# The inverse of a 32x32 triangular factor: four levels of two products against five stages of one, on the tiles of TensorE

## The chip, the cores and the metric

The kernel is one program on one core of a Trainium2 chip. The metric is the device time of one execution in microseconds (us), lower is better. TensorE (PE) multiplies, VectorE (DVE), ScalarE (ACT) and GpSimd (POOL) work element by element, SyncE (SP) issues transfers. Everything is float32.

## What is computed

A time-mixing layer of the RWKV kind over 2 sequences of 4096 tokens with 512 channels, and then eight experts over its 8192 rows. What matters here is the recurrence of each of the 16 heads (width 32):

```python
def step(S, inp):
    r_, w_, k_, v_, kk_, b_ = inp
    sab = jnp.einsum('bhvk,bhk->bhv', S, kk_)
    S = S * jnp.exp(w_)[:, :, None, :] + sab[..., None] * b_[:, :, None, :] + v_[..., None] * k_[:, :, None, :]
    y = jnp.einsum('bhvk,bhk->bhv', S, r_)
    return (S, y)
```

Since `sab` of a token depends on the states of all tokens before it, a chunk of 32 tokens is solved at once: with L the strictly triangular 32x32 matrix of the scores between `kk` and `b`, the inverse of a unit triangular matrix made of L is needed for each head and chunk.

## The kernel before

The program has two parts. `time_mix` runs until about 4600 us of the profile, `experts` after it; the change touches the first alone. `time_mix` takes 128 rows in a turn (64 tokens of each of the two sequences), so there are 64 tiles. Four stages of different tiles share a turn: N and A (norm, projections), B (scores of the tile before), C (solving and the state of the tile before that) and D (output). `LONG` = 28 turns are written out in a loop body that runs twice, with some turns ahead of it and behind it. A turn has 16 units (`U`: 4 channel groups x 2 sequences x 2 chunks), and each unit 4 heads, which lie on the four groups of 32 partitions (`head(h)`). A small product of one head thus takes one 32x32 tile of the PE array, the one in row group h and column group h.

The order of each engine is written by hand. `DVE_STEPS`, `ACT_STEPS`, `POOL_STEPS` and `PE_STEPS` list the steps of a turn, each engine counts them with a semaphore, and `on_vector`, `on_scalar`, `on_gpsimd` and `on_tensor` issue in that order and wait for counts of the others. A name such as C.P0 is a step of stage C. `Banks` lists who uses which of the eight PSUM banks in turn; `clear` waits for the last reader.

The inverse in a turn before:

- Stage B leaves `ub` (L, turned), `invT` (the identity with the first pairs filled in under a mask) and `inv` (`invT` turned).
- For each of four levels, `P_of` (L849) computes 64 products of 32x32 by 32 columns into bank 6, ACT copies them to `part` (L605), `Q_of` (L860) computes 64 more into bank 7, DVE copies those entries that the level adds into `invT` under a mask (L402, C.T) and turns the result into `inv` (L406, C.I; not after the last level). P and Q are each issued in two halves of 32 products with other PE work between.

Every float32 product is two records in the profile, so a half is 64 records. Between the halves stand the steps that the prediction follows: `value_of` (L825), "centre" (L964), "mix" (L972), "rated" (L978), "var" (L990, which reads D.squares of ACT, L644), "delta" (L929), `low` for gate1, low_wa and low_k (L834), `key_of` (L825), the scores u0 to u5 and y0 to y5 (`score`, L874), "decay" (L1053), low2 (L1069) and `from_values` (L888). DVE takes the scores out of PSUM under the mask of known keys (`mask_scores`, L377), into one tile `raw`. D.gated (L484) is the DVE step that frees the bank of u1. PE runs at `from_values` into both banks of the inverse.

## Time and profile before

| | |
|---|---|
| median of 3 runs | 6516.54 us (6496.91 to 6517.45) |
| the profiled execution | 6509.57 us, span of its instructions 6507.4 us |
| PE busy | 5869.2 us (90%), 135752 matrix products |
| DVE busy | 3906.5 us (60%) |
| ACT busy, POOL busy | 1874.9 us (29%), 937.7 us (14%) |
| mean granted TensorE clock | 0.973 of 2.4 GHz |

A busy engine is one with an instruction in flight. A row of the timeline gives when a group of like instructions starts, how long it lasts to the end of its last instruction, and in brackets the idle time before it with who ended it; "issue" stands for idle time for which the profile shows no wait. PE's products overlap, so the time that a group takes of PE is read from its start to the start of the next group.

### The profile page before, as it was taken

How to read it: one execution, taken by the hardware profiler on the slowest of the kernel's cores; microseconds unless marked ns; L12 is line 12 of the kernel's file. 1: busy time of each engine (PE TensorE's matmuls, PEld its weight loads, DVE VectorE, ACT ScalarE, POOL GpSimd, SP SyncE). 2: the span in 40 equal slices, each digit the busy share in tenths (PEclk: the TensorE clock that was granted, in tenths of full speed). 3: DMA queues.
4: the chain of work that ended last, by engine and by line, in shares of the span. 5: the costliest groups of instructions: out<-in, count | busy, mean ns of one | idle time of the engine just before them, and what ended most of it. 6: DMA issues, size and time to landing. Idle time of an engine off the chain costs nothing. (4 is left out here: it accounts for less than half of the span.)

```text
span 6507.4 us, 293913 instructions
## 1 busy us (share of the span) xinstructions
PE 5869.2 (90%) x135752; PEld 4180.8 (64%) x135752; DVE 3906.5 (60%) x9323; ACT 1874.9 (29%) x3531; POOL 937.7 (14%) x900
## 2 busy tenths in 40 slices
PE   6888988998988888898888988987499999999999
PEld 5777777777777777777777777776244444444443
DVE  5777777777777777777777777775523323322300
ACT  3333333333333333333333333332000000000000
POOL 0111111111111111111111111110202202220210
PEclk9999999999999999999999999998699999999999
DMA  1000000000000000000000000000211211121120
GB/s 57 21 18 17 23 17 18 23 17 17 23 17 17 23 18 17 22 19 17 23 18 17 24 17 17 24 15 14 90 46 66 73 65 60 60 92 46 66 71 13
DMA packets 108833, 214.34 MB, mean 33 GB/s; under 512 B 25424, under 2 KB 26704, under 8 KB 107088
## 3 DMA queue, kind: packets, MB, share of 16 engines
q1 hardware_dynamic: 92240, 144.98, 7.6%
q0 software_dynamic: 15360, 50.48, 2.3%
q8 instruction: 1073, 17.58, 1.1%
q14 instruction: 160, 1.31, 0.1%
HBM read 144.67 MB, written 50.72 MB: 30 GB/s over the span
## 5 line engine op out<-in xcount | busy, mean ns | idle before, releaser
L377 DVE COPY_PREDICATED time_raw<-time_known,w_bank 128x96 f32<-128x96 int32 (+6 forms) x3072 | 823.5, 274 | 240.3 <-PE w_bank L874 151.9
L1661 PE MATMUL moe_bank<-moe_w,moe_hidden 128*128 128x512 f32 x2048 | 928.7, 596 | 0.0
L1648 PE MATMUL moe_bank<-moe_hT,moe_w 128*128 128x512 f32 x2048 | 924.8, 594 | 0.8 <-DVE moe_hT L1548 0.8
L1648 PEld LDWEIGHTS moe_bank<-moe_hT,moe_w 128*128 128x128 f32 x2048 | 386.8, 191 | 472.3 <-issue 471.1
L1661 PEld LDWEIGHTS moe_bank<-moe_w,moe_hidden 128*128 128x128 f32 x2048 | 379.4, 190 | 429.5 <-issue 428.1
L1569 ACT ACTIVATE moe_hidden<-moe_bank,moe_b 128x512 f32<-128x512 f32 x256 | 175.9, 687 | 1628.2 <-PE moe_bank L1648 1522.9
L860 PE MATMUL w_bank<-time_invT,time_part 32*32 32x32 f32 x32768 | 418.7, 196 | 141.1 <-issue 88.2
L860 PEld LDWEIGHTS w_bank<-time_invT,time_part 32*32 32x32 f32 x32768 | 372.4, 107 | 201.3 <-issue 138.5
L849 PE MATMUL w_bank<-time_inv,time_ub 32*32 32x32 f32 x32768 | 412.6, 196 | 72.9 <-issue 38.7
L849 PEld LDWEIGHTS w_bank<-time_inv,time_ub 32*32 32x32 f32 x32768 | 355.0, 107 | 190.4 <-issue 149.9
L802 POOL TENSOR_TENSOR time_tail<-time_tail,time_lp 128x512 f32<-128x512 f32 x64 | 75.4, 1178 | 2777.8 <-ACT time_lp L732 2682.9
L874 PE MATMUL w_bank<-time_keys,time_queries_u 32*32 32x160 f32 x8192 | 356.4, 300 | 49.5 <-DVE time_mixed L484 35.0
L874 PE MATMUL w_bank<-time_keys,time_queries_y 32*32 32x160 f32 x8192 | 350.7, 302 | 36.8 <-issue 18.7
L402 DVE COPY_PREDICATED time_invT<-time_levels,w_bank 128x512 f32<-128x512 int32 x256 | 186.9, 730 | 307.4 <-PE w_bank L860 307.2
L1548 DVE COPY moe_hT<-moe_bank 128x512 f32<-128x512 f32 x64 | 44.2, 691 | 535.5 <-PE moe_bank L1635 535.5
L874 PEld LDWEIGHTS w_bank<-time_keys,time_queries_y 32*32 32x32 f32 x8192 | 251.4, 106 | 125.2 <-issue 74.9
L392 DVE SCALAR_TENSOR_TENSOR time_lerp<-w_bank,time_maa,time_xx 128x128 f32<-128x128 f32 x1024 | 284.8, 341 | 54.8 <-PE w_bank L929 54.6
L874 PEld LDWEIGHTS w_bank<-time_keys,time_queries_u 32*32 32x32 f32 x8192 | 239.1, 105 | 89.3 <-DVE time_mixed L484 41.1
L609 ACT COPY time_corr<-w_bank 128x256 f32<-128x256 f32 x128 | 47.6, 372 | 853.6 <-PE w_bank L912 853.6
L825 PE MATMUL w_bank<-time_xf,time_key_w 128*128 128x128 f32 x2048 | 290.6, 292 | 1.8 <-ACT time_part L605 0.7
L825 PE MATMUL w_bank<-time_xf,time_value 128*128 128x128 f32 x2048 | 288.5, 291 | 0.1
L825 PE MATMUL w_bank<-time_xf,time_receptance 128*128 128x128 f32 x2048 | 280.1, 285 | 0.8 <-issue 0.8
(225 smaller groups left out, 9716.9 us busy)
## 6 DMA issues: line engine op xcount, KB each, us to landing
moe_w<-in_w SPq DMA_DIRECT2D x64, 1024.0 KB, 7.2
mid_xn<-time_xn_rows SPq DMA_DIRECT2D x128, 129.0 KB, 2.7
time_x_rows<-in_x SPq DMA_DIRECT2D x128, 128.0 KB, 2.9
time_base<-in_x SPq DMA_DIRECT2D x128, 128.0 KB, 3.2
mid_acc<-time_mixed SPq DMA_DIRECT2D x128, 128.0 KB, 2.7
mid_scores<-time_rated SPq DMA_DIRECT2D x128, 2.0 KB, 1.7
moe_b<-in_b SPq DMA_DIRECT2D x8, 256.0 KB
time_receptance<-in_w_receptance SPq DMA_DIRECT2D x1, 1024.0 KB, 4.9
```

Source lines behind the costliest of these rows:

```text
L377: e.copy_predicated(by_raw[:, "uy".index(q), n0:n1, :, 0:8 * j + 8], known[:, "uy".index(q), :, :, mine].to_broadcast([P, n1 - n0, 2, 8 * ...
L392: e.scalar_tensor_tensor(grp(lerp, g), grp(BANK[f"delta{f}"], g), wt["maa"][:, f * G + g:f * G + g + 1], grp(xx, g), ALU.add, ALU.mult).th ...
L402: e.copy_predicated(chunks(got["invT"]), level(lev + 1, U), chunks(BANK[f"Q{lev}"])).then_inc(dve.sem, dve.step(f"C.T{lev}"))
L609: e.copy(col(corr), BANK[f"solve.{n}{c}"][:, 0:SU * N]).then_inc(act.sem, act.step(f"C.{n}{c}"))
L802: e.tensor_tensor(chunks(tail), chunks(tail), padded(lp)[:, :, 1:33], ALU.add).then_inc(pool.sem, pool.step("A.lt"))
L825: mm = e.matmul(ps[:, o * P:(o + 1) * P], weight[:, g * width + o * P:g * width + (o + 1) * P], rhs_of(g), start=g == 0 and (o == 0 or not ...
L849: mm = e.matmul(BANK[f"P{lev}"][head(h), blk(n)], got["ub"][head(h), blk(n)], got["inv"][head(h), blk(n)], start=True, stop=True, skip_gro ...
L860: mm = e.matmul(BANK[f"Q{lev}"][head(h), blk(n)], part[head(h), blk(n)], got["invT"][head(h), blk(n)], start=True, stop=True, skip_group_c ...
L874: mm = e.matmul(BANK[f"{q}{m}"][head(h), (n - n0) * 2 * KEYS:(n - n0 + 1) * 2 * KEYS], queries[q][head(h), blk(n)], keys[head(h), n * 2 * ...
L1569: e.activation(hidden[now % 4][:, :], up[now % 3][:, :], ACT.Gelu_apprx_tanh, bias=b1[:, x * FC + k:x * FC + k + 1]).then_inc(act.sem, act ...
L1648: got = e.matmul(up[now % 3][:, :], w1[:, g * F + k * P:g * F + (k + 1) * P], hT[x % 2][:, g * CAP + half * HALF:g * CAP + (half + 1) * HA ...
L1661: got = e.matmul(down[t][:, :], hidden[now % 4][:, t * P:(t + 1) * P], tile(w2, k), start=k == 0, stop=k == FC - 1)
```

## The change

The inverse is made by another recurrence. With A the unit triangular matrix and W the inverse so far, the pair [E | W] with E = W A is multiplied from the left by 2I - E, which gives both the next E and the next W. Stage B leaves W = I - L (`sum_of(ew)`, turned from `raw`, whose first quarter now starts as the identity) and 2I - W, which is E for the start (`rest_of(ew)`), the latter on POOL (B.e1). Five stages k = 1, 2, 4, 8, 16 follow. Stage 1 makes E alone (32 moving columns a product), stages 2, 4 and 8 make both (64 columns), stage 16 makes W alone (32 columns). Each stage has 64 products, in two halves again, written over both banks 6 and 7. Between two stages ACT copies the banks to `ew` (C.S), DVE turns the E part into `grow` (C.t), and POOL subtracts it from twice the identity (C.b); the last stage is copied to `invT` by ACT.

In stages 2 and 8 the products of units 8 to 15 write their result two column groups on, and stages 4 and 16 read them there. Their tiles are (row group h, column group h + 2) beside (h, h). The units are issued in the order 0, 8, 1, 9, and so on.

Removed are all P and Q products, `part`, the masks `levels` and their DVE copies, four DVE transposes (three C.I and B.inv), and POOL's copy of the identity (B.eye).

```diff
-            def invert(lev):
-                e.wait_ge(pe.sem, pe[f"C.Q{lev}"])
-                e.copy_predicated(chunks(got["invT"]), level(lev + 1, U), chunks(BANK[f"Q{lev}"])).then_inc(
-                    dve.sem, dve.step(f"C.T{lev}"))
-                if lev < 3:
-                    e.wait_ge(dve.sem, dve[f"C.T{lev}"])
-                    e.transpose(col(got["inv"]), col(got["invT"])).then_inc(dve.sem, dve.step(f"C.I{lev}"))
+            def turn_rest(k):
+                if k == 1 and c_was:
+                    e.wait_ge(pe.old, pe.ago("C.S16"))
+                e.wait_ge(act.sem, act[f"C.S{k}"])
+                e.transpose(chunks(grow), rest_of(got["ew"])).then_inc(dve.sem, dve.step(f"C.t{k}"))
...
+            if Cs:
+                turn_rest(8)
+            if Bs:
                 e.wait_ge(dve.sem, dve["B.u5.3"])
-                e.transpose(col(out["ub"]), raw_of(0)).then_inc(dve.sem, dve.step("B.ub"))
-            if Cs:
-                invert(3)
-            if Bs:
-                e.wait_ge(pool.sem, pool["B.eye"])
-                e.wait_ge(dve.sem, dve["B.ub"])
-                e.copy_predicated(chunks(out["invT"]), level(0, U), chunks(out["ub"])).then_inc(
-                    dve.sem, dve.step("B.pairs"))
-                e.wait_ge(dve.sem, dve["B.pairs"])
-                e.transpose(col(out["inv"]), col(out["invT"])).then_inc(dve.sem, dve.step("B.inv"))
+                e.transpose(sum_of(out["ew"]), chunks(raw_of(0))).then_inc(dve.sem, dve.step("B.ub"))
...
+            def inverse_of(k):
+                e.wait_ge(pe.sem, pe[f"C.S{k}"])
+                if k == 1:
+                    e.copy(rest_of(got["ew"]), rest_of(both_banks)).then_inc(act.sem, act.step("C.S1"))
+                elif k == 16:
+                    e.copy(chunks(invT), sum_of(both_banks)).then_inc(act.sem, act.step("C.S16"))
+                else:
+                    e.copy(col(got["ew"]), inv_bank).then_inc(act.sem, act.step(f"C.S{k}"))
...
+            def grow_of(k):
+                e.wait_ge(dve.sem, dve[f"C.t{k}"])
+                e.tensor_tensor(chunks(grow), every_unit(wt["eye2"]), chunks(grow), ALU.subtract).then_inc(
+                    pool.sem, pool.step(f"C.b{k}"))
...
+            def inverse_stage(k, half):
+                if half == 0:
+                    clear(e, f"S{k}")
+                    clear(e, f"S{k}+")
+                    if k == 1:
...
+                        e.wait_ge(pool.old, pool.ago("B.e1"))
+                    else:
+                        e.wait_ge(pool.sem, pool[f"C.b{k // 2}"])
+                taken = {1: slice(0, N), 16: slice(N, 2 * N)}.get(k, slice(0, 2 * N))
+                by = raw_of(0) if k == 1 else grow
+                for i in range(half * HALF_U // 2, (half + 1) * HALF_U // 2):
+                    for n in (i, i + HALF_U):
+                        turned_in = TURN * (n // HALF_U) * (k in (4, 16))
+                        turned_out = TURN * (n // HALF_U) * (k in (2, 8))
+                        for h in range(HG):
+                            rows, to = head((h + turned_in) % HG), head((h + turned_out) % HG)
+                            mm = e.matmul(both_banks[to, n * 2 * N + taken.start:n * 2 * N + taken.stop], by[rows, blk(n)],
+                                          got["ew"][rows, n * 2 * N + taken.start:n * 2 * N + taken.stop],
+                                          start=True, stop=True, skip_group_check=True)
+                if half:
+                    mm.then_inc(pe.sem, pe.step(f"C.S{k}"))
```

On PE the first place is the start of a turn: mix (L972), rated (L978), the first Q halves (L860) with a part of value (L825) between, var (L990) and delta (L929) before.

```order
L972 MATMUL w_bank<-time_lerp,time_maa_w 128x128 x4
L978 MATMUL w_bank<-time_gcent,time_x 64x8 x8
L860 MATMUL w_bank<-time_invT,time_part 32x32 x32
L825 MATMUL w_bank<-time_xf,time_value 128x128 x4
L860 MATMUL w_bank<-time_invT,time_part 32x32 x32
L990 MATMUL w_bank<-time_sq,time_head_ones 128x512
L929 MATMUL w_bank<-time_mix,time_maa_w 128x128 x12
L825 MATMUL w_bank<-time_hid_g,time_gate_w 128x128 x4
L849 MATMUL w_bank<-time_inv,time_ub 32x32 x32
```

After the change, the same place on PE (mix is L991, rated L997, var L1005, delta L948, a stage's half L879):

```order
L991 MATMUL w_bank<-time_lerp,time_maa_w 128x128 x4
L997 MATMUL w_bank<-time_gcent,time_x 64x8 x8
L847 MATMUL w_bank<-time_xf,time_value 128x128 x4
L1005 MATMUL w_bank<-time_sq,time_head_ones 128x512
L948 MATMUL w_bank<-time_mix,time_maa_w 128x128 x12
L847 MATMUL w_bank<-time_hid_g,time_gate_w 128x128 x4
L879 MATMUL w_bank<-time_ew,time_grow 32x64 x32
```

Both Q halves are gone ahead of var, and the half of P behind the gate has become a half of stage 2 with 64 columns.

The second place is the end of the inverse on PE, from the decay (L1053 before, L1057 after) to the scores y (L874, L894) and from_values (L888, L907). Before:

```order
L1053 MATMUL w_bank<-time_hid_w,time_decay_w 128x128 x4
L849 MATMUL w_bank<-time_inv,time_ub 32x32 x32
L874 MATMUL w_bank<-time_keys,time_queries_u 32x160 x16
L860 MATMUL w_bank<-time_invT,time_part 32x32 x32
L1069 MATMUL w_bank<-time_hid,time_low_w 128x128 x16
L860 MATMUL w_bank<-time_invT,time_part 32x32 x32
L874 MATMUL w_bank<-time_keys,time_queries_y 32x160 x24
L888 MATMUL w_bank<-time_by_values,time_vT 32x96 x32
```

After:

```order
L1057 MATMUL w_bank<-time_hid_w,time_decay_w 128x128 x4
L879 MATMUL w_bank<-time_ew,time_grow 32x64 x32
L894 MATMUL w_bank<-time_keys,time_queries_u 32x160 x16
L879 MATMUL w_bank<-time_ew,time_grow 32x32 x32
L1073 MATMUL w_bank<-time_hid,time_low_w 128x128 x16
L879 MATMUL w_bank<-time_ew,time_grow 32x32 x32
L894 MATMUL w_bank<-time_keys,time_queries_y 32x160 x24
L907 MATMUL w_bank<-time_by_values,time_vT 32x96 x32
```

The order reads alike, but the halves after the scores u4 and u5 (L894, x16) are now stage 16, which reads `grow` of stage 8, where the halves of Q3 read `part` of ACT.

The third place is POOL over a turn. Before (L780 B.rk, L783 B.eye, L771 the queries, L767 C.faded, L802 A.lt, L808 and L813 B.us and B.ys):

```order
L780 TENSOR_TENSOR time_rk<-time_r,time_k 128x512 [waits mix_go_pool,pe_steps2,dve_steps2,act_steps2,pool_steps2]
L783 COPY time_invT<-time_eye 128x512 [waits pe_steps2]
L771 TENSOR_TENSOR time_queries_u<-time_dq,time_kkn 128x512 [waits pe_steps2,dve_steps2,act_steps3]
L771 TENSOR_TENSOR time_queries_y<-time_dq,time_r 128x512 [waits pe_steps2,act_steps2,act_steps3]
L767 TENSOR_TENSOR time_faded<-time_state,time_decay_end 128x256 [waits act_steps2,dve_steps2]
L802 TENSOR_TENSOR time_tail<-time_tail,time_lp 128x512 [waits act_steps3]
```

After:

```order
L796 TENSOR_TENSOR time_rk<-time_r,time_k 128x512 [waits mix_go_pool,pe_steps2,dve_steps2,act_steps2,pool_steps2]
L787 TENSOR_TENSOR time_queries_u<-time_dq,time_kkn 128x512 [waits pe_steps2,dve_steps2,act_steps3]
L783 TENSOR_TENSOR time_grow<-time_eye,time_grow 128x512 [waits dve_steps3]
L787 TENSOR_TENSOR time_queries_y<-time_dq,time_r 128x512 [waits pe_steps2,act_steps2,act_steps3]
L778 TENSOR_TENSOR time_faded<-time_state,time_decay_end 128x256 [waits act_steps2,dve_steps2]
L783 TENSOR_TENSOR time_grow<-time_eye,time_grow 128x512 [waits dve_steps3] x3
L820 TENSOR_TENSOR time_ew<-time_eye,time_ew 128x16x32 [waits dve_steps3]
L824 TENSOR_TENSOR time_tail<-time_tail,time_lp 128x512 [waits act_steps3]
```

POOL has lost the copy of the identity and has four subtractions into `grow` (L783) and one into `ew` (L820); the first stands ahead of the y queries.

## Rows read from the trace of the kernel before

**Rows 1.** The page, DMA queues: the queue of instructions, packets, MB, share

```profile
q8 instruction: 1073, 17.58, 1.1%
```

**Rows 2.** One line's instructions (L953, a turn's first), 674 to 4310 us

```profile
L953 PE MATMUL w_bank<-time_ident,time_xn_rows x212: 272/273/445, 674.5 to 4300.1; 128*128 128x128 f32 x106
```

**Rows 3.** Timeline of PE, one turn: start, length, work, [idle before <-releaser]

```profile
2853.30 1.12 PE L990 MATMUL w_bank<-time_sq,time_head_ones 128*128 128x512 f32 x2
...
2865.81 1.02 PE L874 MATMUL w_bank<-time_keys,time_queries_u 32*32 32x160 f32 x24 [0.66 <-DVE time_mixed L484]
2867.28 0.74 PE L849 MATMUL w_bank<-time_inv,time_ub 32*32 32x32 f32 x64 [0.46 <-DVE time_inv L406]
2869.01 1.13 PE L834 MATMUL w_bank<-time_xf,time_low_k 128*128 128x128 f32 x8 [0.99 <-DVE time_xf L398]
2870.07 0.75 PE L849 MATMUL w_bank<-time_inv,time_ub 32*32 32x32 f32 x64
2870.76 2.05 PE L825 MATMUL w_bank<-time_xf,time_key_w 128*128 128x128 f32 x16
```

**Rows 4.** Timeline of PE, the end of the inverse in that turn

```profile
2879.75 0.60 PE L849 MATMUL w_bank<-time_inv,time_ub 32*32 32x32 f32 x47
2881.33 0.34 PE L849 MATMUL w_bank<-time_inv,time_ub 32*32 32x32 f32 x17 [0.98 <-issue]
2881.51 1.29 PE L874 MATMUL w_bank<-time_keys,time_queries_u 32*32 32x160 f32 x32
2882.60 0.78 PE L860 MATMUL w_bank<-time_invT,time_part 32*32 32x32 f32 x64
2883.34 0.71 PE L1069 MATMUL w_bank<-time_hid,time_low_w 32*128 32x128 f32 x12
2884.92 0.94 PE L1069 MATMUL w_bank<-time_hid,time_low_w 32*128 32x128 f32 x20 [0.87 <-issue]
2885.79 0.75 PE L860 MATMUL w_bank<-time_invT,time_part 32*32 32x32 f32 x64
2886.40 2.39 PE L874 MATMUL w_bank<-time_keys,time_queries_y 32*32 32x160 f32 x48
2888.57 1.55 PE L888 MATMUL w_bank<-time_by_values,time_vT 32*32 32x96 f32 x64
```

**Rows 5.** Timeline of PE: 64 records of 64 columns on four tiles

```profile
2903.99 1.09 PE L902 MATMUL w_bank<-time_by_state,time_state 32*32 32x64 f32 x64
2905.01 2.05 PE L825 MATMUL w_bank<-time_xf,time_receptance 128*128 128x128 f32 x16
```

**Rows 6.** Timeline of DVE, the same turn

```profile
2842.94 1.33 DVE L423 TENSOR_TENSOR time_grown<-time_grown,time_shrink 128x256 f32<-128x256 f32 x1
2844.30 0.71 DVE L427 TENSOR_TENSOR time_state<-time_grown,time_faded 128x256 f32<-128x256 f32 x1
...
2865.67 0.72 DVE L402 COPY_PREDICATED time_invT<-time_levels,w_bank 128x512 f32<-128x512 int32 x1
2866.42 0.71 DVE L406 STREAM_TRANSPOSE time_inv<-time_invT 128x512 f32<-128x512 f32 x1
...
2882.32 2.07 DVE L377 COPY_PREDICATED time_raw<-time_known,w_bank 128x32 f32<-128x32 int32 x8 [1.30 <-PE w_bank L874]
...
2900.97 0.43 DVE L423 TENSOR_TENSOR time_grown<-time_grown,time_shrink 128x256 f32<-128x256 f32 x1
```

**Rows 7.** Timeline of ACT, the same turn

```profile
2850.77 0.58 ACT L644 ACTIVATE time_sq<-w_bank 128x512 f32<-128x512 f32 x1
...
2886.87 0.61 ACT L702 ACTIVATE time_thmk<-w_bank 128x512 f32<-128x512 f32 x1
```

**Rows 8.** Timeline of POOL, the same turn

```profile
2852.00 1.19 POOL L771 TENSOR_TENSOR time_queries_u<-time_dq,time_kkn 128x512 f32<-128x512 f32 x1 [7.26 <-ACT time_dq L647]
```

**Rows 9.** Busy time by windows: PE, PEld, DVE, ACT, POOL, then PE's granted clock

```profile
2003.60:2007.00 3.40, 2.43 (x55) 2.02 (x42) 3.40 (x8) 0.96 (x2) 0.00 (x0) 1.00 0.00 0
2007.00:2010.40 3.40, 3.11 (x80) 2.86 (x84) 2.20 (x7) 2.86 (x6) 0.58 (x1) 0.50 0.02 5
```

More of the change, by code:

```diff
@@ L214, in time_mix @@
         eights = lambda t: t[:, :].rearrange("p (n j s) -> p n j s", n=U, j=BLOCKS)
-        level = lambda i, n: wt["levels"][:, blk(i)].rearrange("p (o t) -> p o t", o=1).to_broadcast([P, n, N])
+        every_unit = lambda t: t[:, :].rearrange("p (o t) -> p o t", o=1).to_broadcast([P, U, N])
+        pairs_of = lambda t: t[:, :].rearrange("p (n s t) -> p n s t", n=U, s=2)
+        rest_of = lambda t: pairs_of(t)[:, :, 0]
+        sum_of = lambda t: pairs_of(t)[:, :, 1]
+        inv_bank = both_banks[:, :]
         FILLS = {"x": x, "lp": lp, "state": state, "raw": raw, "bank4": psum[4], "bank5": psum[5]}
-        dve.stage([*FILLS, "pad", "hid_w", "ones"] + [f"bonus_ones{g}" for g in range(G)]
+        dve.stage([*FILLS, "pad", "hid_w", "ones", "raw_eye"] + [f"bonus_ones{g}" for g in range(G)]
                   + [f"bias_ones{g}" for g in range(G)] + ["gcent", "offset"])
@@ L459, in on_vector @@
             if Cs:
-                invert(0)
+                turn_rest(1)
             if A:
@@ L780, in on_gpsimd @@
                 e.tensor_tensor(col(rk), col(r), col(k2), ALU.mult).then_inc(pool.sem, pool.step("B.rk"))
-                if "C.y1" in pe.was:
-                    e.wait_ge(pe.old, pe.ago("C.y1"))
-                e.tensor_copy(chunks(out["invT"]), wt["eye"][:, :].rearrange("p (o t) -> p o t", o=1).to_broadcast(
-                    [P, U, N])).then_inc(pool.sem, pool.step("B.eye"))
                 e.wait_ge(act.sem, act["B.eq"])
@@ L799, in on_gpsimd @@
                 faded_of(0)
+                grow_of(2)
+                grow_of(4)
+                grow_of(8)
+            if Bs:
+                e.wait_ge(dve.sem, dve["B.ub"])
+                e.tensor_tensor(rest_of(out["ew"]), every_unit(wt["eye2"]), sum_of(out["ew"]), ALU.subtract).then_inc(
+                    pool.sem, pool.step("B.e1"))
             if A:
@@ L845, in P_of @@
                     else:
-                        e.wait_ge(dve.sem, dve[f"C.I{lev - 1}"])
-                for n in range(half * U // 2, (half + 1) * U // 2):
-                    for h in range(HG):
-                        mm = e.matmul(BANK[f"P{lev}"][head(h), blk(n)], got["ub"][head(h), blk(n)], got["inv"][head(h), blk(n)],
-                                      start=True, stop=True, skip_group_check=True)
-                if half:
-                    mm.then_inc(pe.sem, pe.step(f"C.P{lev}"))
@@ L854, in Q_of @@
-            def Q_of(lev, half):
-                if half == 0:
-                    clear(e, f"Q{lev}")
-                    e.wait_ge(act.sem, act[f"C.P{lev}"])
-                for n in range(half * U // 2, (half + 1) * U // 2):
-                    for h in range(HG):
-                        mm = e.matmul(BANK[f"Q{lev}"][head(h), blk(n)], part[head(h), blk(n)], got["invT"][head(h), blk(n)],
-                                      start=True, stop=True, skip_group_check=True)
-                if half:
-                    mm.then_inc(pe.sem, pe.step(f"C.Q{lev}"))
+                        e.wait_ge(pool.sem, pool[f"C.b{k // 2}"])
@@ L1171, in time_mix_inputs @@
     t = row % N
-    same = lambda size: t // size == i // size
-    upper = {h: same(2 * h) & (t // h == i // h - 1) for h in (1, 2, 4, 8, 16)}
     f32 = lambda a: np.ascontiguousarray(a.astype(np.float32))
```

102 lines of the change are left out of this document (45 added, 57 removed), and 8 rows, old and new, of the table DVE_STEPS.

## The prediction, made before the changed kernel ran

> **What bounds the kernel now.** I read the rows of a turn's first line [rows 2], the timeline of each engine over one turn, and the windows with the granted clock. 212 records of L953, four to a turn, are 53 turns; (4300.1 - 0.4 - 674.5) / 52 = 69.7 us is a turn. I walk through the one that starts at 2841.18, 69.1 us long. From from_values on, at 2888.57 [rows 4], PE runs nearly without a wait to the end of the turn. Before it, PE meets waits: for D.gated ahead of u1 (0.66), for the turned inverse (0.46), for a mixed input (0.99) [rows 3], and "issue" gaps of 0.98 and 0.87 [rows 4]. Between resuming at 2881.33 and stopping at 2884.05 pass 2.7 us, so dense small products outrun the fetch. So PE bounds the end of the turn, and a chain over all engines its first two thirds. A saving on PE counts only where that chain gets shorter too.
>
> **What PE saves.** A half with 32 columns is 64 records in 2870.76 - 2870.07 = 0.69 us [rows 3]. Before there are 16 halves: 11.0 us. After there are 10. Four (stages 1 and 16) have 32 columns: 2.8 us. Six have 64 columns, which the trace shows on four tiles alone: 2905.01 - 2903.99 = 1.02 us [rows 5]. On eight tiles no row shows them. The lower end is half of 1.02, 0.51, if the tiles are all that counts; but 32 columns, half the streaming of 64, took 0.69 and not 0.51, so something per record holds as well. I take 0.69, the rate at which PE already gets through 64 records. That makes 4.1, and the sum 6.9 us: 4.1 less a turn. With 1.02 it is 8.9: 2.1 less.
>
> The pages speak both ways here. In the Trainium skill, "TensorE: Matmul & The Clock Gate", Part 3 (The mechanism), a weight load overlaps a product in flight only if it goes to another row group; the added tiles share their row groups with the old ones, so by that rule nothing would be gained from them, and six halves would stay at 1.02. Its section on measured speedup has sixteen tiles 10.6 times as fast as one, rows and columns together. No row here settles it; the rule is the first rival.
>
> **The chain, joint by joint.** Times are those of the turn in the rows, on eight tiles.
>
> *var.* POOL's copy of the identity is gone. L427 took 0.71 beside it, and the same kind of add over 256 columns takes 0.43 (L423, alone) [rows 6], so DVE runs 0.3 earlier into the mixing. With both Q halves gone, PE reaches var at about 2849.8, but var reads the squares of ACT, over at 2850.77 + 0.58 = 2851.35 [rows 7], now 0.3 earlier: var starts at 2851.15 instead of 2853.30 [rows 3], 2.15 earlier, behind a wait of 1.3.
>
> *u1.* From var to D.gated nothing of the chain (delta, the inputs, low_wa, ACT's affine) gets shorter: it moves 2.15. The first subtraction of POOL (1.19, as L771 [rows 8]) is over before the gate's products are, and costs nothing. Two POOL operations beside DVE cost something: L423 took 1.33 beside POOL's first operation of the turn and 0.43 alone [rows 6]; a DVE operation with both inputs in SBUF seems to wait for POOL. The first input's add (L398) falls on the y queries and loses some 0.6, still ahead of its use. u1 starts at 2863.6 instead of 2865.81. Q1a and Q1b no longer lie around u0, so PE waits about 2 us there in sum.
>
> *Stage 4.* Before, P starts 1.5 after D.gated is over (copy 0.72, transpose 0.71, latency). Now a transpose and a subtraction, 0.65 + 1.2, precede it: 1.9. It starts at 65.5 instead of 67.28 [rows 3], 1.8 earlier.
>
> *u4.* From there to u4 were 2881.51 - 2867.28 = 14.2 us. Two Q halves go (1.4), the wait of 0.99 goes as the input now comes first, the issue gap of 0.98 goes as the dense stretch is thinner, and a wait of 0.3 for POOL ahead of stage 8 is new: 11.1. u4 starts at 76.6, 4.9 earlier.
>
> *Stage 16: the new wait.* Q3 started at once behind u5 [rows 4], since ACT had its input. Stage 16 needs `grow` of stage 8, and C.t8 stands on DVE behind all masks of u4 and u5. These end 2882.32 + 2.07 - 2881.51 = 2.9 after u4 starts [rows 4, 6]; then transpose (0.65) and subtraction (1.2) with latencies: 4.85. PE has 1.1 us of scores for that time and idles 3.7 us. Queued behind are stage 16, low2, all y scores and from_values. Stage 16 starts at 81.45 instead of 2882.60: of 4.9 us, 1.15 are left.
>
> *from_values.* Before, 2888.57 - 2882.60 = 6.0 us passed for Q3a, low2, Q3b, y0 and y1 [rows 4], with a gap of 0.87 in low2 and more in the scores. Without gaps a half takes 0.69, low2 some 1.2 (20 of its 32 records took 0.87), and y0 and y1 1.63 (32 records of u4 and u5 took 1.09, these are 48): 4.2 in sum. ACT's last copy stands behind three activations (to 2887.48 [rows 7], 1.7 after low2) and ends 2.2 after low2, as PE does. from_values would start at 85.65, 2.9 earlier. After the long wait the next packet of instructions has been fetched, but four more dense groups follow; I give back 0.65 for gaps: 2.25 us a turn. Behind it everything moves along; the freed 2.9 us of DVE and ACT's longer copies (over two banks) lie beside PE.
>
> **The clock.** In 2003.6 to 2007.0 PE was busy 2.43 of 3.40 us, and in the next 3.4 us it was granted 0.50, 1.2 instead of 2.4 GHz; over the whole execution the mean is 0.973, so some 5% of the time is at half clock already [rows 9]. With 3.7 us idle in one piece each turn, and 2 to 3 us around u0, u1 and stage 4, I expect such a stretch about every turn behind the first and in half of the turns at the second. One of 3.4 us costs up to 1.7 where PE binds, less where the wait or a gap of the fetch covers it: 0.7 and 0.5 on average, 1.2 in sum. The skill's same page, Part 1, likewise lets idle stretches bring the clock down, and the rows agree (0.50 after 2.43 busy of 3.40).
>
> **Sum.** 2.25 - 1.2 = about 1.0 us a turn, over 64 turns 64 us. From the profiled execution's own 6509.6 us that is 6445; it is 7 us below the median, so I forecast 6452 us for the median, 1.0% faster.
>
> **Rivals.**
> 1. *The added tiles don't run beside the old ones.* Six halves at 1.02 instead of 0.69, all on the chain (two before low_wa, two around low_k, two ahead of u4): 2.0 us a turn more, minus 1.0 becomes plus 1.0: 6516 + 64 = 6580 us, 1% slower. It decides as soon as a 64-column half takes over 0.86 us. For it: no row shows two tiles on one row group, and a page's rule. Against it: nothing in the rows.
> 2. *The waits cost what PE saves.* If the clock falls in every turn at both places with its full 1.7, hardly covered, 3.4 instead of 1.2 is paid, and the gain is over: about 6520 us. For it: 2.43 us busy of 3.40 were few enough. Against it: the second stretch lies before a wait that partly absorbs it.
> 3. *PE binds all the way.* If the waits that I count are covered (the profile's 90% busy PE speaks for it), all 4.1 us arrive: 64 x 4.1 = 262 us, 6254 us. Against it: C.t8 cannot come before the masks of u5.
> 4. *No clock loss.* The chain as walked with 2.25 us: 6516 - 144 = 6372 us.
>
> **Numbers.** Forecast with its surroundings (6400 to 6495): 0.45; rival 1: 0.25; rival 2: 0.14; rival 3: 0.05; rival 4: 0.11. The range that leaves out rival 3 and the tails is 6365 to 6590. A measurement of this kernel tells some 0.3% from no change, so faster means below 6497 and slower above 6536: 0.58 faster, 0.14 the same, 0.28 slower.
>
> **What would show it.** Stage halves with 64 columns 0.6 to 0.7 us apart (rival 1: 1.0). PE idle ahead of stage 16 near 3.7 us, released by POOL's subtraction; ahead of var near 1.3, released by ACT's squares. from_values 44 to 46 us after the turn's first record instead of 47.4. Mean clock of the execution 0.95 to 0.97 instead of 0.973. A turn of 68.7 us instead of 69.7. Wrong it would be if the subtractions on POOL take much longer than 1.2 us, if the issue gaps stay as before, or if the clock stays low for long stretches.

## The result: 2.1% slower, and the profile after

| | before | after |
|---|---|---|
| median | 6516.99 us (6496.91 to 6521.21, 4 runs) | 6649.51 us (6633.48 to 6659.95, 4 runs) |
| ratio, 95% interval | | 1.0207 [1.0177, 1.0238] |
| span of the profiled execution | 6507.4 us | 6631.5 us |
| PE busy | 5869.2 us, 135752 products | 5824.3 us, 111176 products |
| DVE, ACT, POOL busy | 3906.5, 1874.9, 937.7 us | 3675.6, 1990.0, 1312.2 us |
| mean granted clock | 0.973 | 0.925 |

The forecast was 6452 us with a range of 6365 to 6590, so the sign was wrong and the time lies outside the range. 24576 PE records are gone and PE's busy time has hardly moved. Before any explanation, the place: the two kernels differ in the turns alone. The first line of a turn, one row of each kernel (min/median/max length, first and last start):

```profile
L953 PE MATMUL w_bank<-time_ident,time_xn_rows x256: 272/273/472, 32.0 to 4370.1; 128*128 128x128 f32 x128
```

```profile
L972 PE MATMUL w_bank<-time_ident,time_xn_rows x256: 272/273/473, 31.7 to 4491.7; 128*128 128x128 f32 x128
```

The last turn starts 121.6 us later, of 124.1 us that the span is longer. Over 63 turns that is 1.93 us a turn; the forecast had 1.0 us less.

The waits of PE that ended between 700 and 4300 us, in the kernel after (line that waited, who released it: us in total, times, longest):

```profile
PE w_bank L879 <- POOL time_grow L783: 233.4, 150, 3.7
PE w_bank L894 <- DVE time_mixed L493: 93.8, 51, 1.8
PE w_bank L1005 <- ACT time_sq L652: 63.9, 50, 1.4
PE w_bank L879 <- issue: 25.6, 45, 1.1
...
PE w_bank L847 <- ACT time_sq L658: 10.9, 38, 0.3
```

The first row is a stage that waits for POOL's subtraction, 150 times in 50 turns, the longest 3.7 us: the wait before stage 16. The second is u1 waiting for D.gated, the third "var" waiting for the squares. All three were named ahead, with about these sizes. So the waits alone don't explain the loss, and one has to go through a turn. Timeline of PE in the kernel after, one turn that starts at 2698.47 (rows between them left out):

```profile
2708.48 1.10 PE L1005 MATMUL w_bank<-time_sq,time_head_ones 128*128 128x512 f32 x2 [1.39 <-ACT time_sq L652]
...
2710.96 1.16 PE L847 MATMUL w_bank<-time_hid_g,time_gate_w 128*128 128x128 f32 x8 [0.29 <-ACT time_sq L658]
2712.05 0.85 PE L879 MATMUL w_bank<-time_ew,time_grow 32*32 32x64 f32 x64
2712.83 1.16 PE L847 MATMUL w_bank<-time_xf,time_value 128*128 128x128 f32 x8
...
2718.66 1.02 PE L894 MATMUL w_bank<-time_keys,time_queries_u 32*32 32x160 f32 x24
2721.52 1.82 PE L894 MATMUL w_bank<-time_keys,time_queries_u 32*32 32x160 f32 x24 [1.84 <-DVE time_mixed L493]
2723.57 1.17 PE L879 MATMUL w_bank<-time_ew,time_grow 32*32 32x64 f32 x64 [0.23 <-POOL time_grow L783]
2724.67 2.08 PE L856 MATMUL w_bank<-time_xf,time_low_k 128*128 128x128 f32 x8
2726.67 1.18 PE L879 MATMUL w_bank<-time_ew,time_grow 32*32 32x64 f32 x64
...
2736.87 1.29 PE L894 MATMUL w_bank<-time_keys,time_queries_u 32*32 32x160 f32 x32
2741.84 1.03 PE L879 MATMUL w_bank<-time_ew,time_grow 32*32 32x32 f32 x64 [3.67 <-POOL time_grow L783]
2742.79 2.09 PE L1073 MATMUL w_bank<-time_hid,time_low_w 32*128 32x128 f32 x32
2744.81 0.68 PE L879 MATMUL w_bank<-time_ew,time_grow 32*32 32x32 f32 x40
2745.74 0.43 PE L879 MATMUL w_bank<-time_ew,time_grow 32*32 32x32 f32 x24 [0.24 <-issue]
2745.95 3.10 PE L894 MATMUL w_bank<-time_keys,time_queries_y 32*32 32x160 f32 x48
2748.86 1.34 PE L907 MATMUL w_bank<-time_by_values,time_vT 32*32 32x96 f32 x56
```

Three things stand in it. A half with 64 columns on eight tiles takes 2712.83 - 2712.05 = 0.78 us. Behind the wait of 1.84 everything is slow: the same 24 records of scores take 1.82 instead of the 1.02 of the row above, low_k 2.00 us instead of 1.06 [rows 3]. Behind the wait of 3.67 it is the same, with low2 at 2.02 and the y scores at 2.91. The windows of this turn (PE, PEld, DVE, ACT, POOL busy, then PE's granted clock) name the cause:

```profile
2721.30:2728.10 6.80, 6.35 (x161) 4.96 (x162) 6.47 (x20) 0.84 (x3) 1.25 (x1) 0.50 0.01 2
2728.10:2741.80 13.70, 9.56 (x248) 8.15 (x247) 8.21 (x26) 3.48 (x5) 2.64 (x3) 1.00 0.01 3
2741.80:2748.60 6.80, 6.52 (x201) 5.69 (x205) 0.60 (x3) 3.65 (x8) 1.11 (x1) 0.50 0.02 5
```

In this turn PE was granted 1.2 GHz instead of 2.4 for 6.8 us behind each of the two long waits. Over the 58 turns from the fifth to the 62nd there is such a stretch in 57 turns at the first place and in all 58 at the second. They last 3.4 or 6.8 us, a few 10.2: per turn 5.0 us at the first place and 6.3 at the second. In all it is 12.5 us a turn against 2.5 before. The forecast had foreseen a stretch "about every turn" at the first place and in half of the turns at the second, and took one of 3.4 us for its price [rows 9].

The chain behind the wait of 3.67, on DVE and on POOL:

```profile
2737.68 2.07 DVE L387 COPY_PREDICATED time_raw<-time_known,w_bank 128x32 f32<-128x32 int32 x8 [0.96 <-PE w_bank L894]
2739.65 0.70 DVE L415 STREAM_TRANSPOSE time_grow<-time_ew 128x512 f32<-128x512 f32 x1
```

```profile
2740.43 1.26 POOL L783 TENSOR_TENSOR time_grow<-time_eye,time_grow 128x512 f32<-128x512 f32 x1 [6.23 <-DVE time_grow L415]
```

Masks of u4 and u5, transpose, subtraction, as walked ahead: u4 at 2736.87, stage 16 at 2741.84.

**The joints.** Where the groups of a turn start, in us into the turn, averaged over the fifth to the 62nd turn of each kernel (58 turns). Single turns differ, so that a mean at the late joints is known to some 0.2 us. The third column is the move that the prediction gave, before its 1.2 for the clock:

| | before | after | forecast | measured |
|---|---|---|---|---|
| var | 11.42 | 9.97 | -2.15 | -1.45 |
| low_wa | 19.27 | 18.53 | -2.15 | -0.74 |
| stage 4 (P of the third level) | 25.75 | 25.51 | -1.8 | -0.24 |
| u4 | 39.81 | 38.59 | -4.9 | -1.22 |
| stage 16 (Q of the last level) | 41.55 | 43.65 | -1.15 | +2.10 |
| from_values | 47.55 | 50.22 | -2.25 | +2.67 |
| end of the turn | 69.69 | 71.68 | -2.25 | +1.99 |

The rest of the turn, behind from_values, became 0.7 us shorter (22.14 and 21.46); PE's idle time in it fell from 0.9 to 0.4 us. The loss against the forecast lies in four joints: ahead of var, var to low_wa, stage 4 to u4, and stage 16 to from_values.

### The profile page after: what moved, and what is told of

It is laid out like the page before. It is cut to its first block and busy times, and to the rows that moved or that the text cites. A ratio compares the mean times of both kernels' runs of the same rounds, so it can differ in the third digit from the quotient of the medians.

```text
span 6631.5 us, 244569 instructions
## 1 busy us (share of the span) xinstructions
PE 5824.3 (88%) x111176; PEld 4057.1 (61%) x111176; DVE 3675.6 (55%) x9004; ACT 1990.0 (30%) x3595; POOL 1312.2 (20%) x1156
## 5 line engine op out<-in xcount | busy, mean ns | idle before, releaser
L879 PE MATMUL w_bank<-time_ew,time_grow 32*32 32x64 f32 x32768 | 482.9, 243 | 334.0 <-POOL time_grow L783 310.0
L879 PEld LDWEIGHTS w_bank<-time_ew,time_grow 32*32 32x32 f32 x32768 | 395.8, 120 | 456.4 <-issue 429.7
L783 POOL TENSOR_TENSOR time_grow<-time_eye,time_grow 128x512 f32<-128x512 f32 x256 | 323.0, 1262 | 1580.9 <-DVE time_grow L415 1580.9
L894 PE MATMUL w_bank<-time_keys,time_queries_u 32*32 32x160 f32 x8192 | 378.3, 317 | 121.7 <-DVE time_mixed L493 113.3
L894 PE MATMUL w_bank<-time_keys,time_queries_y 32*32 32x160 f32 x8192 | 407.1, 344 | 16.9 <-DVE time_mixed L553 12.1
L894 PEld LDWEIGHTS w_bank<-time_keys,time_queries_y 32*32 32x32 f32 x8192 | 294.2, 123 | 116.9 <-issue 50.3
L894 PEld LDWEIGHTS w_bank<-time_keys,time_queries_u 32*32 32x32 f32 x8192 | 244.1, 110 | 189.9 <-DVE time_mixed L493 133.2
L847 PE MATMUL w_bank<-time_xf,time_key_w 128*128 128x128 f32 x2048 | 273.6, 289 | 0.0
L847 PEld LDWEIGHTS w_bank<-time_xf,time_key_w 128*128 128x128 f32 x2048 | 249.6, 199 | 23.8 <-issue 20.5
L963 PE MATMUL w_bank<-time_output,time_mixed 128*128 128x512 f32 x512 | 256.0, 623 | 3.9 <-DVE time_mixed L493 3.9
```

The costliest lines, as they stand in the source:

```text
L783: e.tensor_tensor(chunks(grow), every_unit(wt["eye2"]), chunks(grow), ALU.subtract).then_inc(pool.sem, pool.step(f"C.b{k}"))
L847: mm = e.matmul(ps[:, o * P:(o + 1) * P], weight[:, g * width + o * P:g * width + (o + 1) * P], rhs_of(g), start=g == 0 and (o == 0 or not ...
L879: mm = e.matmul(both_banks[to, n * 2 * N + taken.start:n * 2 * N + taken.stop], by[rows, blk(n)], got["ew"][rows, n * 2 * N + taken.start: ...
L894: mm = e.matmul(BANK[f"{q}{m}"][head(h), (n - n0) * 2 * KEYS:(n - n0 + 1) * 2 * KEYS], queries[q][head(h), blk(n)], keys[head(h), n * 2 * ...
L963: mm = e.matmul(BANK["out"][:, :], grp(mixed, g), wt["output"][:, g * C:(g + 1) * C], start=g == 0, stop=g == G - 1)
```

## Experiments

Theory at this point: the tiles work and the waits are as forecast, but the price of the clock was put too low, and behind the wait for stage 16 PE runs at the pace of its instruction fetch, which the time saved ahead doesn't shorten. Rivals: the added tiles bring nothing; the clock alone; POOL as the culprit. Times are compared within the kernels that share their runs of the kernel before, or by the ratios to it (1% is 65 us). Averages are over the same 58 turns.

**e1_four_tiles**: the tiles of before, all else as changed.

```diff
-TURN = 2
+TURN = 0
```

> The changed kernel with all units on the tiles (h, h): the turn by two column groups is set to 0, so four tiles instead of eight. In the trace of the changed kernel a half with 64 columns takes 0.78 us on eight tiles, against 1.02 for such products on four. My theory (the tiles do run side by side, and the six halves lie on the chain) expects halves of 1.02 to 1.05 us and 6 x 0.25 = 1.5 us a turn more, less what the waits ahead of u1 and stage 8 absorb: 0.8 to 1.5 us over 64 turns, 50 to 95 us slower than the changed kernel (6700 to 6745 us). The rival, that the halves are bound by something else than the tiles or lie in the waits' cover, expects no change (within 15 us).

Measured: 6735.18 us, ratio 1.0301 [1.0283, 1.0318], 0.94% above the changed kernel (61 us; between the profiled executions 102 us). The first stage with 64 columns and the group behind it, timeline of PE:

```profile
1752.10 1.10 PE L879 MATMUL w_bank<-time_ew,time_grow 32*32 32x64 f32 x64
1753.13 1.16 PE L847 MATMUL w_bank<-time_xf,time_value 128*128 128x128 f32 x8
```

1.03 us a half, as rows 5 had it, against 0.78 on eight tiles. So the second set of tiles does run beside the first, and rival 1 of the prediction falls. The Trainium skill ("TensorE: Matmul & The Clock Gate", Part 3, The mechanism) has weight loads overlap with products in flight only where the row group differs; read strictly, eight tiles would have stayed at 1.03, and these two kernels don't agree with it. They don't reach half of 1.03 either. The loss is within the 50 to 95 us that were expected.

**e2_fill16** and **e3_fill_both**: PE gets unused products during its waits, which need no data that is late, so that it isn't idle there. e2 puts three products of 512 columns ahead of stage 16; e3 has in addition 512 and 256 columns between u0 and u1. Nothing else changes; their results are never read.

```diff
+            def fill(*columns):
+                clear(e, "mk")
+                for n in columns:
+                    e.matmul(BANK["mk"][:, 0:n], wt["head_ones"][:, :], xf[0][:, 0:n], start=True, stop=True)
...
+                if A and Cs:
+                    fill(512, 256)
...
+            if A and Cs:
+                fill(512, 512, 512)
```

> The changed kernel with three products of 128x128 by 128x512 (1.06 us each) into an idle PSUM bank, their results unused, put on PE into the wait of 3.67 us ahead of stage 16. They add no work to the chain. Theory clock: the wait itself was forecast right; what came on top is the half clock that follows it. Then low2 goes from 2.02 to about 1.1 us, y0 and y1 from 2.8 to 1.7, and the kernel gains 1.5 to 2.2 us a turn, 95 to 140 us (6510 to 6555 us). Theory wait: the time behind the wait is late input or fetch of instructions, which the added products leave or make worse: no gain, or up to 30 us slower.

> As the run before, and in addition one product with 512 and one with 256 columns (1.6 us) between u0 and u1, where PE waits 1.84 us. Theory clock: the second half-clock stretch of a turn, from u1 to the key product, goes too: stage 4's halves from 1.1 to 0.78 us, low_k from 2.0 to 1.1, about 1.3 us a turn and 60 to 90 us less than the run before (6430 to 6490 us), the mean clock over the turns back at 0.97 or more. Theory wait: no change against the run before.

Measured: e2 6638.43 us, 1.0168 [1.0135, 1.0202]; e3 6569.53 us, 1.0045 [1.0028, 1.0062]. Half clock falls from 12.5 us a turn to 8.3 and 3.4. e2 is only 25 us faster than the changed kernel by the ratios, where 95 to 140 were expected, and the two intervals overlap; e3 is 69 us faster than e2, as expected. The same clock is worth much at one place and little at the other. At stage 4, e3's half takes 0.77, low_k 1.09, and from stage 4 to u4 pass 11.9 us instead of e2's 13.4. Behind stage 16, the timeline of PE in e2 shows what takes the clock's place:

```profile
1948.05 0.74 PE L879 MATMUL w_bank<-time_ew,time_grow 32*32 32x32 f32 x64 [0.91 <-POOL time_grow L783]
1948.76 1.17 PE L1080 MATMUL w_bank<-time_hid,time_low_w 32*128 32x128 f32 x32
1949.87 0.35 PE L879 MATMUL w_bank<-time_ew,time_grow 32*32 32x32 f32 x30
1951.44 0.46 PE L879 MATMUL w_bank<-time_ew,time_grow 32*32 32x32 f32 x34 [1.23 <-issue]
1951.72 1.86 PE L894 MATMUL w_bank<-time_keys,time_queries_y 32*32 32x160 f32 x48
1953.37 1.17 PE L907 MATMUL w_bank<-time_by_values,time_vT 32*32 32x96 f32 x44
1955.41 0.68 PE L907 MATMUL w_bank<-time_by_values,time_vT 32*32 32x96 f32 x20 [0.88 <-issue]
```

Stage 16 and low2 now run at full speed (0.71 and 1.11), and then PE stands twice, "issue" 1.23 and 0.88, with 34 + 48 + 44 = 126 records between the two gaps: the packet of 125 records that the prediction had counted. From resuming to resuming pass 1955.41 - 1951.44 = 3.97 us, in rows 4 it was 2884.92 - 2881.33 = 3.59. Averaged over the turns, stage 16 to from_values is 5.96 us in e2 and 6.56 in the changed kernel, so 0.6 us are gained there. But PE idles 1.2 us of these 5.96, where it was 0.2 of 6.56, and behind from_values the gain is lost again: from stage 16 to the end of the turn pass 27.9 us in e2 and 28.0 in the changed kernel.

**e6_before_long**: does the fetch set the pace there in the kernel before, too? The second half of the last Q (64 records) is replaced by one product of 512 columns (2 records). Half of the last level is not computed.

```diff
-                Q_of(3, 1)
+                e.matmul(BANK["Q3"][:, :], wt["head_ones"][:, :], col(part), start=True, stop=True).then_inc(
+                    pe.sem, pe.step("C.Q3"))
```

> The kernel before with the second half of Q3 (32 products, 64 records, 0.69 us of PE) left out and one product of 128x128 by 128x512 (2 records, 1.06 us of PE) in its place; the last level of the inverse is so not computed. Theory fetch: in the dense stretch from P3 to the output product PE gets a packet of some 250 instructions (125 records with their weight loads) every 3.5 to 3.6 us, whatever they do, so 62 records less are 1.7 us less there: 0.8 to 1.6 us a turn, 50 to 100 us faster than before. Rival, PE's own work sets the pace there: 0.37 us a turn more, 24 us slower than before.

Measured: 6449.57 us, ratio 0.9896 [0.9864, 0.9927], 68 us faster, although 1.06 us of array work stand where 0.69 stood. Q3 to from_values takes 5.4 us instead of 6.0, and Q3 to the end of the turn 26.8 instead of 28.1. Fewer instructions are worth more there than less work for the array.

**e9_after_long** and **e10_fill16_long**: two limits could each hold the stretch behind stage 16, the half clock and the fetch. The same replacement of the second half of stage 16, once in the changed kernel (the half clock stays) and once in e2 (full clock). Half of the last level is not computed in either.

```diff
-                inverse_stage(16, 1)
+                e.matmul(BANK["S16"][:, :], wt["head_ones"][:, :], col(grow), start=True, stop=True).then_inc(
+                    pe.sem, pe.step("C.S16"))
```

> The changed kernel with the second half of stage 16 (64 records and their weight loads, 0.98 us) replaced by one product of 512 columns (2 records), so half of the last level is not computed. It has the fewer instructions behind the wait before stage 16, but the stretch at half clock is still there. If the fetch of instructions alone paces the stretch from stage 16 to from_values (6.6 us), it gets about 62 of 128 records' worth of fetching shorter, 1.2 to 1.8 us a turn: 75 to 115 us less than the changed kernel, a ratio to the kernel before of 1.003 to 1.009. If the half clock paces it as much as the fetch does, the long product takes some 2.1 us there (the 512 columns of low_k at half clock took 2.08) instead of 0.98, and from_values comes up to 1.1 us later: between 20 us less and 70 us more, 1.018 to 1.031.

> The same replacement in the kernel whose wait before stage 16 is filled with unused products (1.0168 there): half of the last level is not computed, the clock is full behind the wait, and the fetch has 62 records less. If the fetch was what kept that kernel from gaining, stage 16 to from_values takes 4.6 to 5.2 us instead of 6.7, and the time falls by 95 to 135 us: 0.996 to 1.002. If a third thing paced that stretch (masks, copies of ACT), nothing comes: 1.013 to 1.018.

Measured: e9 6655.48 us, ratio 1.0185 [1.0168, 1.0202], no difference that can be told from the changed kernel. e10 6517.39 us, 0.9963 [0.9945, 0.9981], 0.0205 below e2, 134 us. PE in e9, then in e10:

```profile
1750.30 0.90 PE L879 MATMUL w_bank<-time_ew,time_grow 32*32 32x32 f32 x64 [3.69 <-POOL time_grow L783]
1751.14 2.09 PE L1073 MATMUL w_bank<-time_hid,time_low_w 32*128 32x128 f32 x32
1753.16 2.08 PE L1077 MATMUL w_bank<-time_grow,time_head_ones 128*128 128x512 f32 x2
1755.17 2.28 PE L894 MATMUL w_bank<-time_keys,time_queries_y 32*32 32x160 f32 x48
1757.28 1.49 PE L907 MATMUL w_bank<-time_by_values,time_vT 32*32 32x96 f32 x64
```

```profile
714.46 0.74 PE L879 MATMUL w_bank<-time_ew,time_grow 32*32 32x32 f32 x64 [0.90 <-POOL time_grow L783]
715.17 1.17 PE L1080 MATMUL w_bank<-time_hid,time_low_w 32*128 32x128 f32 x32
716.27 1.13 PE L1084 MATMUL w_bank<-time_grow,time_head_ones 128*128 128x512 f32 x2
717.33 1.83 PE L894 MATMUL w_bank<-time_keys,time_queries_y 32*32 32x160 f32 x48
718.98 1.50 PE L907 MATMUL w_bank<-time_by_values,time_vT 32*32 32x96 f32 x64
```

In e9 low2 and the long product stand at 2.0 us each, half speed. In e10 the five groups follow each other without a gap, and from_values starts 718.98 - 714.46 = 4.5 us behind stage 16. Over the turns, in us:

| | stage 16 to from_values | PE's idle time in it | stage 16 to the end of the turn |
|---|---|---|---|
| changed kernel | 6.56 | 0.2 | 28.0 |
| e2, clock given back | 5.96 | 1.2 | 27.9 |
| e9, fewer instructions | 7.15 | 0.2 | 28.4 |
| e10, both | 4.85 | 0.2 | 26.2 |

Neither alone brings the end of the turn forward, both together bring it 1.8 us forward. That is why neither experiment alone moved the time. With the full clock alone PE waits for instructions instead; at half clock the array's work fills nearly all of the 6.6 us. e9 is not a clean test: its long product takes 2.0 us at half clock where the half took 0.95 in the turn read above. Taking these 1.05 off the 28.4 gives, as an estimate, 27.35, so fewer instructions alone may be worth up to 0.7 us a turn, against 1.7 at full clock (e2 to e10).

**e4_reorder**: something useful in the wait instead. low2 and the scores y0 and y1 go ahead of stage 16, both its halves follow in one piece, then the sums and from_values; ACT takes the squares for the sums ahead of its last copy. All is computed.

```diff
-            "B.u1 A.low_k C.S4 B.u2 A.key B.u3 A.decay C.S8 B.u4 B.u5 A.low2 C.S16 B.y0 B.y1 A.sums C.z0 B.y2 "
+            "B.u1 A.low_k C.S4 B.u2 A.key B.u3 A.decay C.S8 B.u4 B.u5 A.low2 B.y0 B.y1 C.S16 A.sums C.z0 B.y2 "
...
-            "A.thmk C.S16 A.sq N.xn B.e0 B.decay_end ...
+            "A.thmk A.sq C.S16 N.xn B.e0 B.decay_end ...
```

> The changed kernel with another order behind the scores u4 and u5: low2, y0 and y1 run on PE in the wait, then both halves of stage 16, then sums and from_values (the square that sums reads is made by ACT ahead of its last copy). All work as in the changed kernel. The forecast's chain says that 2.7 us of PE work then lie in the wait of 3.67: from_values starts 3 to 4.5 us earlier in a turn, and with a wait of 1 us or less the clock stays up there: 200 to 290 us faster than the changed kernel (6360 to 6450 us), faster than the kernel before. If the clock alone made the loss, it gains as much as the run with the three added products. If PE's order isn't what holds stage 16 up, nothing.

Measured: 6475.16 us, ratio 0.9914 [0.9891, 0.9938], 0.9% faster than the kernel before and 2.9% (191 us by the ratios) below the changed one, somewhat less than the 200 to 290 expected. from_values starts 46.9 us into the turn instead of 50.2, as expected, but the rest of the turn is 0.75 us longer, although the sums have left it. The wait before stage 16 is 0.8 us in the turn read. The fetch still shows: PE has issue gaps there, and its idle time behind the start of from_values is 1.8 us a turn instead of 0.4.

**e5_reorder_affine**: e4, and ACT's affine of stage D (L686) goes ahead of the three activations of low inputs that it stood behind, so that D.gated comes earlier and u1 waits less.

```diff
-... B.v C.S2 A.hid_g A.hid_w A.hid_a D.affine0 D.affine1 D.affine2 D.affine3 A.hid_kkk
+... B.v C.S2 D.affine0 D.affine1 D.affine2 D.affine3 A.hid_g A.hid_w A.hid_a A.hid_kkk
```

> As e4_reorder, and in addition ACT does its four D.affine operations (1.65 us) ahead of hid_g, hid_w and hid_a instead of behind them, where it idled 1.0 us. So D.gated, and with it u1 and stage 4, come 1.4 us earlier; the wait of 1.84 us ahead of u1 shrinks to about 0.4. Chain theory: 1.4 us a turn, 90 us less than e4_reorder; clock theory in addition: the half-clock stretch from u1 to the key product (4 to 5 us a turn at half clock in e4_reorder) mostly goes, another 1.0 us a turn: 90 to 150 us less in sum, 0.969 to 0.978 of the kernel before. Rival, that PE's instructions set the pace of the turn as a whole: under 20 us.

Measured: 6278.96 us, ratio 0.9628 [0.9597, 0.9658], clock 0.968. PE at the same place as above:

```profile
2252.95 1.02 PE L894 MATMUL w_bank<-time_keys,time_queries_u 32*32 32x160 f32 x24 [0.27 <-DVE time_mixed L493]
2254.99 0.84 PE L879 MATMUL w_bank<-time_ew,time_grow 32*32 32x64 f32 x64 [1.03 <-POOL time_grow L783]
2255.77 1.16 PE L856 MATMUL w_bank<-time_xf,time_low_k 128*128 128x128 f32 x8
```

The wait before u1 is 0.27 instead of 1.84, and nothing behind it runs at half speed. u0 to stage 4 is 3.0 us instead of 4.9 in e4, and stage 4 to u4 11.9 instead of 13.2. So 1.6 us of waiting had cost 1.3 more behind it, by the clock. In sum it is 186 us by the ratios, more than the 90 to 150 expected: both terms came out larger than the 1.4 and 1.0 us a turn of the expectation.

**e7_dve_sub**: POOL as the culprit. In the changed kernel DVE makes the four subtractions itself, each right behind its transpose. And **e8_all**: e5 with them.

```diff
-            "B.rk B.qu C.b1 B.qy C.faded0 C.b2 C.b4 C.b8 B.e1 A.lt B.us C.faded1 B.ys").split()
+            "B.rk B.qu B.qy C.faded0 B.e1 A.lt B.us C.faded1 B.ys").split()
...
+                e.wait_ge(dve.sem, dve[f"C.t{k}"])
+                e.tensor_tensor(chunks(grow), every_unit(wt["eye2"]), chunks(grow), ALU.subtract).then_inc(
+                    dve.sem, dve.step(f"C.b{k}"))
```

> The changed kernel with the four subtractions from twice the identity between stages on DVE (0.69 us, right behind the transpose) instead of POOL (1.26 us and a handover). Chain theory: stages 4, 8 and 16 start 0.5 to 0.6 us earlier each, 1.0 to 1.6 us a turn if nothing else holds; theory fetch: what stage 16 gains is given back behind it, so 0.5 to 1.1 us a turn remain, 30 to 70 us faster than the changed kernel. Rival, that DVE's four more operations (2.8 us a turn) delay its masks as much: no gain.

> e5_reorder_affine and e7_dve_sub together: the version that is to beat both kernels. If the two add up, 30 to 60 us less than e5_reorder_affine, 0.960 to 0.972 of the kernel before. Theory fetch: the stretch from stage 8 to the output product stays near 15 us and what comes earlier before it is kept, since the whole turn moves forward.

Measured: e7 6580.79 us, ratio 1.0089 [1.0055, 1.0123], 77 us below the changed kernel by the ratios (30 to 70 expected); e8 6226.43 us, 0.9551 [0.9522, 0.9581], 52.5 us below e5 (30 to 60 expected) and 4.5% below the kernel before. A subtraction takes 0.69 us on DVE where POOL took 1.26. That was a part of the loss, but without it the kernel is still slower than before, at a clock of 0.927. In e8 the waits on the inverse's subtractions are small, 0.4 us at most. Between 700 and 4100 us PE's largest waits in sum are var's for the squares and issue gaps, and the longest single one of those shown is an issue gap of 2.7 us:

```profile
PE w_bank L998 <- ACT time_sq L655: 65.1, 51, 1.4
PE w_bank L872 <- issue: 52.9, 56, 2.7
...
PE w_bank L872 <- DVE time_grow L417: 22.7, 60, 0.4
```

## Why the prediction was wrong

**What held.** The waits: ahead of var 1.39 (1.3 forecast), around u0 1.84 (about 2), ahead of stage 16 3.67 (3.7), u4 to stage 16 5.06 on average (4.85). POOL's subtraction took 1.26 (1.2). Eight tiles run side by side. The mechanism, clock and fetch against a saving on PE, was the right one; the sizes were not, and the starting point was not. With them the sign came out wrong.

**The clock, 1.2 us a turn.** This is one of the two mis-sized terms that weigh most. It rested on a stretch of 3.4 us at 0.50 in about every turn at the first place and in half of them at the second, and measured were 5.0 and 6.3 us a turn. At u1 and stage 4 it costs, by the rows of the turn read, 0.8 in the scores, 0.3 in the half, 0.9 in low_k and 0.3 in the second half, and by the runs 1.3 to 1.5 us a turn between stage 4 and u4 (e2 against e3: 13.4 and 11.9; e4 against e5: 13.2 and 11.9). The scores' 0.8 was hidden: PE then waited for POOL 0.23 instead of 1.03 (e5). The forecast had 0.7 here. Behind stage 16 the clock acts together with the fetch, below.

**from_values, 4.2 + 0.65 from stage 16.** Measured 6.56. "After the long wait the next packet of instructions has been fetched, but four more dense groups follow; I give back 0.65 for gaps" is the other step that failed, together with the 0.5 for the clock at this place. At full clock the stretch takes 5.96 with 1.2 us idle, and what is gained there is lost behind from_values (e2); without the gaps it is 4.85 (e10, with a product of 1.06 for the half of 0.7), near the forecast. At half clock the array's own work takes most of those 6.6 us. Rows 4 had the figure needed: 125 records between two resumptions in 3.59 us, and stage 16, low2 and the first y scores hold 64 + 32 + 64 + 48 = 208 records. 208 / 125 x 3.59 = 6.0 us, close to what e2 has. The forecast had the packet and its records in its first part and did not use their pace in the sum.

**var, -2.15.** Measured -1.45 against the average, although the place was hit (9.97 on average, and 9.97 in the walk). The turn that was walked had var at 12.12, behind an issue gap that this row of the kernel before shows, in the second half of a Q that is removed:

```profile
2852.76 0.61 PE L860 MATMUL w_bank<-time_invT,time_part 32*32 32x32 f32 x47 [1.19 <-issue]
```

In 30 of the 58 turns var starts 11.8 to 13.0 us into the turn, in the others at 9.8 to 11.2. The saving was taken from a turn with the gap, and so 0.7 us of it was never there on average.

**u1, "nothing of the chain (delta, the inputs, low_wa, ACT's affine) gets shorter: it moves 2.15".** From var to low_wa it became 0.7 us longer (7.85 to 8.56 on average). Of that, 0.5 lies ahead of the gate's product, which meets a wait that it did not have, 0.29 in the row above. Its bank is freed by the activation of ACT that reads var (L658), and ahead of that ACT loads a table:

```profile
2708.93 1.28 ACT L658 ACT_TABLE_LOAD   x1
2710.22 0.69 ACT L658 ACTIVATE time_sq<-w_bank,time_cols 128x512 f32<-128x512 f32 x1
```

In the turn of rows 3, var started behind the Q halves, when this load was over, and the activation 1.16 us behind var (at 2854.46). Now it starts 2710.22 - 2708.48 = 1.74 us behind var. The other 0.2 lies in the two halves with 64 columns, 0.78 and more, where two P halves stood.

**The halves, 0.69.** 0.78 in the rows, on 64 columns and eight tiles: up to 0.09 too little for each of six, at most 0.5 us a turn, and 0.5 instead of 0.3 of waiting before stage 8. Nearest was the value of the forecast, not rival 1.

**The account.** Terms that came out worse than forecast: base of var 0.7, var to low_wa 0.7, the rest up to stage 4 0.15, stage 4 to u4 2.1 (of it 1.3 to 1.5 the clock), stage 16 to from_values 1.7; better: 0.4 between u4 and stage 16, 0.7 behind from_values. In sum 4.2, less the 1.2 that the forecast had for the clock: 3.0. -1.0 + 3.0 = +2.0 us a turn, as the table has it; the first and last turns' starts give 1.93.

**Rival 2**, "the waits cost what PE saves", is nearest to what happened: 1.3 to 1.5 at stage 4 and the 1.7 that clock and fetch share behind stage 16 are near its 3.4 us a turn. But its time doesn't follow from its price: 2.25 - 3.4 = -1.15 us a turn is a loss of 74 us, so 6590 us and not "about 6520". Summed rightly, the rival reached the upper end of the range, and the measured 6649.51 lies 60 us above it; the starting point, the joint to low_wa and the halves are behind that rest. Its argument against itself, that a wait absorbs part of the second stretch, held for the scores' 0.8 at the first place alone.

How the 1.7 behind stage 16 divides between clock and fetch has no answer: each covers most of the other (e2, e9, e10). Why the half clock lasts 6.8 us in some turns and 3.4 in others stays open. That the gaps are the fetch of instructions is inferred from the packets' size, the fixed spacing of the gaps and e6 and e10; no row shows a packet arriving.

## What to carry to other kernels

A wait of PE of 1.8 us cost it 1.3 to 1.5 us again, since the products behind it ran at half clock; the wait of 3.7 us cost nothing more that giving back the clock alone could recover, since the fetch stood behind it. So after an edit that makes PE's work less dense, price the products behind each wait at half clock too, or move independent products into the wait, as e4 did. Where small products follow each other, count the instructions between two gaps and put their pace (here 3.6 to 4.0 us for 125 records) into the sum as a limit beside the array's, because time saved ahead of such a stretch doesn't shorten it. Read such gaps on the whole turn: in e2 a joint became 0.6 us shorter and the turn didn't. And when an experiment that lifts one limit brings nothing, lift the other with it before calling either innocent; take the starting point of a sum from an average over turns, not from one.

## What the runs showed of the hardware

- Two tiles of one row group, in different column groups, overlap: 64 records with 64 columns in 0.78 us instead of 1.03 (e1). With 32 columns 64 records take 0.69 on four tiles.
- Two limits of nearly the same size can lie on one stretch, here from stage 16 to the end of the turn: 28.0 us (both), 27.9 (fetch alone), 28.4 (half clock, with 1.05 us more work), 26.2 (neither).
- PE's issue gaps stand at a fixed spacing of 125 to 128 records of products, or a whole multiple of it: 258 of 259 distances in the kernel before. Two gaps that are one spacing apart lie 3.3 to 6.8 us from each other there, 3.9 in the median.
- A half with 64 columns took 1.10 us from start to start at half clock and 0.78 at full, not twice as long, while 128-column products double (low_k 2.00 and 1.06).
- DVE's add of two SBUF inputs (L408) took 1.21 us beside POOL's operations and 0.69 without, both in the two rows of the changed kernel below. The Trainium skill ("SBUF — State Buffer", Who interferes with whom) has such a DVE instruction contend with a POOL instruction that reads SBUF; the rows agree.

```profile
2711.89 1.21 DVE L408 TENSOR_TENSOR time_xf<-time_lerp,time_x 128x512 f32<-128x512 f32 x1
...
2714.89 0.69 DVE L408 TENSOR_TENSOR time_xf<-time_lerp,time_x 128x512 f32<-128x512 f32 x1
```
